# Cross-attention on one core: some scheduled steps moved to other tiles and engines, and the output projection of 14 batches done as three fp16 products

## The reference

```
q = (x @ Wq + bq).reshape(b, ql, H, D_Q)
k = (ctx @ Wk + bk).reshape(b, kl, H, D_Q)
v = (ctx @ Wv + bv).reshape(b, kl, H, D_Q)
scores = einsum('bqhd,bkhd->bhqk', q, k) / sqrt(D_Q)
attn = softmax(scores, axis=-1)
c = einsum('bhqk,bkhd->bqhd', attn, v).reshape(b, ql, H * D_Q)
z = x + (c @ Wo + bo)
out = (z - mean(z)) * rsqrt(var(z) + 1e-5) * gamma + beta
```

## Time and profile before

| | |
|---|---|
| three runs | 945.15 us median (942.49 to 946.78) |
| the profiled execution | 943.91 us, span of the trace 942.0 us |
| mean granted TensorE clock | 0.989 |
| PE busy | 892.3 us, 95% |
| DVE busy | 830.2 us, 88% |
| ACT busy | 754.6 us, 80% |
| POOL busy | 281.9 us, 30% |

### The profile page before, as it was taken

How to read it: one execution, slowest core, us unless ns; L and a number is a source line. 1 busy time by engine, 2 the same in 40 slices (tenths; PEclk the granted TensorE clock), 3 DMA queues, 4 the chain that set the end, 5 groups by cost and what they waited for, 6 DMA issues and landing times.

```text
span 942.0 us, 25453 instructions
## 1 busy us (share of the span) xinstructions
PE 892.3 (95%) x10366; PEld 673.4 (71%) x10366; DVE 830.2 (88%) x1072; ACT 754.6 (80%) x1082; POOL 281.9 (30%) x368
## 2 busy tenths in 40 slices
PE   7797998999999999999999999999999999999996
PEld 6475876777777776777777777777777676677775
DVE  4897889999898999989799998989999798998983
ACT  3675978888888888888888878888888888888983
POOL 3051394413214141232404223141412424042001
PEclk9998999999999999999999999999999999999999
DMA  8676999999999999999999999999999999999995
GB/s 224 133 159 143 186 175 163 204 203 187 220 181 205 201 214 205 201 213 183 208 198 206 211 178 211 193 215 201 197 212 192 198 196 196 198 183 203 204 178 112
DMA packets 683065, 181.17 MB, mean 192 GB/s; under 512 B 654596, under 2 KB 682052, under 8 KB 682948
## 3 DMA queue, kind: packets, MB, share of 16 engines
q1 hardware_dynamic: 681332, 178.48, 99.3%
q10 hardware_dynamic: 1344, 0.53, 0.2%
q0 software_dynamic: 272, 0.53, 0.2%
HBM read 15.35 MB, written 0.82 MB: 17 GB/s over the span
## 4 chain that ended last, share of the span: by engine, by line
PE 51%; DVE 22%; issue 8%; DMA 8%; POOL 5%; ACT 4%; SPq 1%; POOLq 0%; DVEq 0%; ACTq 0%
PE ps L530 21%; PE ps L544 15%; DVE p_lo L765 9%; PE ps L549 8%; DVE nmax L750 8%; DMA pt_lo<-p_lo 7%; PE ps L399 4%; PE ps L393 2%; DVE c_max L670 1%; ACT p L868 1%; POOL c_lo L975 1%; POOL early_sb L1003 1%; ACT c_hi L850 1%; POOL c_scaled L1001 1%; ACT o_t L891 1%
## 5 line engine op out<-in xcount | busy, mean ns | idle before, releaser
L765 DVE SCALAR_TENSOR_TENSOR p_lo<-p,rinv,p_hi 128x1444 f16<-128x1444 f32 x200 | 352.3, 1762 | 19.5 <-DMA pt_lo<-p_lo 17.2
L868 ACT ACTIVATE p<-ps,nmax 128x1446 f32<-128x1446 f32 x200 | 292.2, 1461 | 89.8 <-DVE nmax L750 89.1
L750 DVE TENSOR_REDUCE nmax<-ps 128x1 f32<-128x1446 f32 x200 | 331.5, 1658 | 36.3 <-PE ps L530 32.6
L876 ACT ACTIVATE p_hi<-p,rinv 128x1444 f16<-128x1444 f32 x200 | 299.8, 1499 | 39.0 <-DVE rinv L758 37.5
L544 PE MATMUL ps<-pt_hi,c_hi 128*128 128x128 f16 (+1 forms) x2288 | 270.0, 217 | 27.9 <-ACT o_t L891 25.2
L544 PEld LDWEIGHTS ps<-pt_hi,c_hi 128*128 128x128 f16 x2288 | 216.0, 98 | 76.2 <-ACT o_t L891 64.1
L544 PE MATMUL ps<-pt_hi,c_lo 128*128 128x128 f16 (+1 forms) x2288 | 269.3, 217 | 0.0
L544 PEld LDWEIGHTS ps<-pt_hi,c_lo 128*128 128x128 f16 x2288 | 217.5, 98 | 12.0 <-issue 0.2
L530 PE MATMUL ps<-ct_hi,g_hi 128*128 128x482 f16 (+3 forms) x624 | 157.2, 370 | 2.1 <-DMA ct_hi<-c_hi 2.1
L549 PE MATMUL ps<-pt_lo,c_hi 128*128 128x128 f16 (+1 forms) x2288 | 157.5, 217 | 0.0
L530 PE MATMUL ps<-ct_hi,g_lo 128*128 128x482 f16 (+3 forms) x624 | 157.1, 370 | 0.0
(11 more groups left out here) (108 smaller groups left out, 654.0 us busy)
## 6 DMA issues: line engine op xcount, KB each, us to landing
c_raw<-in_ctx_dram SPq DMA_DIRECT2D x32, 256.0 KB
pt_hi<-p_hi SPq DMA_TRANSPOSE x200, 3.5
pt_lo<-p_lo SPq DMA_TRANSPOSE x200, 3.7
c_raw<-in_ctx_dram SPq DMA_DIRECT2D x16, 192.0 KB
c_raw<-in_ctx_dram SPq DMA_DIRECT2D x48, 18.0 KB
out_dram<-y SPq DMA_DIRECT2D x16, 50.0 KB
x_sb<-in_x_dram SPq DMA_DIRECT2D x1, 600.0 KB
o_t<-in_L_xattn_Wq_dram SPq DMA_DIRECT2D x2, 256.0 KB, 4.4
```

What stands on the lines that cost most here:

```text
L750: dve.tensor_reduce(nmax[:, n % RING:n % RING + 1], ps[:, bank:bank + 3, 0:KEYW], AX.XY, ALU.max, negate=True).then_inc(s_nm, 1)
L765: dve.scalar_tensor_tensor(out=p_lo[:, par, 0:KL], in0=p32[:, n % P32S, 0:KL], scalar=rinv[:, i:i + 1], in1=p_hi[:, par, 0:KL], op0=ALU.mu ...
L868: act.activation(p32[:, n % P32S, :].rearrange("p (k w) -> p k w", w=KEYW), ps[:, bank:bank + 3, 0:KEYW], ACT.Exp, bias=nmax[:, i:i + 1], ...
L876: act.activation(p_hi[:, par, 0:KL], p32[:, n % P32S, 0:KL], ACT.Copy, scale=rinv[:, i:i + 1]).then_inc(s_hi, 1)
```

## The change

1. **Places.** CMAX_AT goes from 8 to 6. CHI_AT goes from 4, 5, 6 to 4, 6, 7. The context transposes go from r = 6 and 7 to 7 and 8, and the lo transpose to 9 in the first window only. TOP_AT goes from 11 to 10, except in the first window.
2. **Order on ACT.** `take_result(n-4)` is issued ahead of `exponentials(n)`.
3. **Engines.** The row norm (zn) goes from DVE to POOL. `context_scale` loses one small DVE instruction: the least maximum is a fourth column of `c_max`, and the range factor lies in a second identity, `ident_part`.
4. **Output projection.** For batches 1 to 14, `project_out_16` makes per head three fp16 products of a result (hi, lo) and `m_sb` (hi, lo) in place of one fp32 product. The result copy scales by a constant, and the scales are put back in `take_rows`. POOL splits each batch's result in four groups (`split_results`), between its splits of the queries. Once only, DVE takes the maxima of `m_sb` (n = 17 to 20, 22), ACT makes its high part (n = 23 to 26) and POOL its low part. `m16` and `o16` lie in the memory of `a_sb` and `xT`; the norm's tiles lie in that of `wo_sb`.

```
-    CHI_AT = 4
+    CHI_AT = (4, 6, 7)
-    CMAX_AT = 8
-    CT_HI_AT = 6
-    CT_LO_AT = 7
+    CMAX_AT = 6
+    CT_HI_AT = 7
+    CT_LO_AT = 8
+    CT_LO_AT_FIRST = 9
-    TOP_AT = 11
+    TOP_AT = 10
+    TOP_AT_FIRST = 11
...
+            def project_out_16(bank, heads):
+                for h in heads:
+                    rows = slice(QL * h, QL * (h + 1))
+                    for i, j in ((0, 0), (1, 0), (0, 1)):
+                        mm = pe.matmul(bank[0:QL, 0:D], o16[:, i, rows], m16[:, h, j, :], start=(h == 0 and i == j),
+                                       stop=(h == H - 1 and j == 1))
+                return mm
...
+                    if in_parts(w - 1):
+                        pe.wait_ge(s_os, NG * (w - 2) + g + 1)
+                        mm = project_out_16(bank, range(HG * g, HG * (g + 1)))
+                    else:
+                        mm = project_out(bank, (w - 1) % 2, range(HG * g, HG * (g + 1)))
...
-                dve.tensor_reduce(c_top[:, :], bank[:, 0:P], AX.X, ALU.max).then_inc(s_ctop, 1)
-                dve.wait_ge(s_ctop, b + 1)
...
-                dve.tensor_scalar(un, c_top[:, :], C_LEAST, 1.0 / C_RANGE, ALU.max, ALU.mult).then_inc(s_us, 1)
+                dve.tensor_reduce(un, bank[:, 0:P], AX.X, ALU.max).then_inc(s_us, 1)
...
+            def m_parts_max(g):
...
+                dve.tensor_reduce(m_parts[:, g:g + 1], m_sb[:, HG * g:HG * g + HG, :].rearrange("p h e -> p (h e)"), AX.X,
+                                  ALU.max, apply_absolute_value=True).then_inc(s_mp, 1)
...
+                if in_parts(b):
+                    dve.wait_ge(s_fu, b)
+                    dve.scalar_tensor_tensor(out=z[:, par, :], in0=ps[0:QL, JOB_BANK, 0:D], scalar=fin_un[0:QL, par:par + 1],
+                                             in1=x_sb[:, b, :], op0=ALU.mult, op1=ALU.add).then_inc(s_z, 1)
...
-                if r == TOP_AT and w > 0:
-                    norm_rows(w - 1)
...
             for n in range(N + LAG):
+                if n >= LAG:
+                    take_result(n - LAG)
                 if n < N:
                     exponentials(n)
-                if n >= LAG:
-                    take_result(n - LAG)
...
+                    act.activation(m16[:, HG * g:HG * g + HG, 0, :], m_sb[:, HG * g:HG * g + HG, :], ACT.Copy,
+                                   scale=m_scale[:, :]).then_inc(s_mh, 1)
...
+            def split_results(b, g):
+
+                pool.wait_ge(s_ot, results(b, HG * QL * (g + 1)))
+                if g == 0 and b > 1:
+                    pool.wait_ge(s_fin, b)
+                cols = query_columns(g)
+                pool.tensor_copy(o16[:, 0, cols], o_t[:, b % 2, cols]).then_inc(s_oh, 1)
+                pool.wait_ge(s_oh, NG * (b - 1) + g + 1)
+                pool.tensor_tensor(o16[:, 1, cols], o_t[:, b % 2, cols], o16[:, 0, cols], ALU.subtract).then_inc(s_os, 1)
...
+                        if w == 2:
+                            leave_m_lo(g)
+                        if g < NG - 1 and in_parts(w - 1):
+                            split_results(w - 1, g)
                         split_queries(b, g)
...
+                    split_results(w - 1, NG - 1)
+                    output_scale(w - 1)
```

More of the change, by code:

```diff
@@ L16 @@
 AX_RANGE = 2.0 ** 14
+O_PART = 2.0 ** -5
 P_RANGE = 2.0 ** 14
@@ L92, in halves, with results, in_parts @@
         return 16 * (n // 2 + 1)
+    def results(b, rows):
+        for n in range(first_tile(b), last_tile(b) + 1):
+            for i, (owner, row, count, at) in enumerate(segments(n)):
+                if owner == b and row + count >= rows:
+                    return segments_before(n) + i + 1
+    def in_parts(b):
+        return 0 < b < B - 1
     with ExitStack() as es:
@@ L118, in cross_attention_kernel @@
             "p (b i q) -> p b i q", i=2, q=QL)
-        wo_sb = sb("wo_sb", [P, PAIRS, P])
+        late_sb = sb("late_sb", [P, PAIRS, P])
+        wo_sb = late_sb
+        z, zn, zg, y = [late_sb[0:QL, 2 * i:2 * i + 2, :] for i in range(4)]
         bv_sb = sb("bv_sb", [P, PAIRS])
@@ L192, in cross_attention_kernel @@
         s_xres = sem("residual_ready")
+        s_mp = sem("m_group_max")
+        s_mc = sem("m_partition_max")
+        s_mt = sem("m_max_spread")
+        s_ma = sem("m_max")
+        s_mu = sem("m_unscale_ready")
+        s_ms = sem("m_scale_ready")
+        s_mh = sem("m_hi_ready")
+        s_mw = sem("m_scaled")
+        s_ml = sem("m_split")
+        s_oh = sem("result_hi_ready")
+        s_os = sem("result_split")
+        s_fu = sem("output_unscale_ready")
         s_axz = sem("ax_parts_zeroed")
+        s_cleast = sem("least_context_max_set")
         s_ax = sem("ax_group_max")
@@ L255, in cross_attention_kernel @@
         X16_AT = 18
+        MPARTS_AT = 17
+        MTOP_AT = IN_PAIR // 2 + TOP_AT
+        M16_AT = MTOP_AT + 1
         WARM_UP = 12
@@ L358, in _ @@
                     transpose_context_hi(w + 1)
-                if r == CT_LO_AT and w + 1 < B:
+                if r == (CT_LO_AT if w else CT_LO_AT_FIRST) and w + 1 < B:
                     transpose_context_lo(w + 1)
@@ L816, in _ @@
                     parts_max(n - PARTS_AT)
-                if r == TOP_AT and w > 0:
-                    norm_rows(w - 1)
-                if r == TOP_AT and w + 2 < B:
+                if r == (TOP_AT if w else TOP_AT_FIRST) and w + 2 < B:
                     context_scale(w + 2, ps[:, JOB_BANK, :])
@@ L903, in _ @@
                 w, r = window(n)
-                if CHI_AT <= r < CHI_AT + NT and w + 1 < B:
-                    context_hi(w + 1, r - CHI_AT)
+                if r in CHI_AT and w + 1 < B:
+                    context_hi(w + 1, CHI_AT.index(r))
                 for k in ONCE.get(n, ()):
@@ L1021, in _ @@
                     for g in range(NG):
+                        if w == 2:
+                            leave_m_lo(g)
+                        if g < NG - 1 and in_parts(w - 1):
+                            split_results(w - 1, g)
                         split_queries(b, g)
+                    if w == 2:
+                        pool.wait_ge(s_ml, NG)
+                if in_parts(w - 1):
+                    if b == B:
+                        for g in range(NG - 1):
+                            split_results(w - 1, g)
+                    split_results(w - 1, NG - 1)
+                    output_scale(w - 1)
+                if b < B:
                     if w == 1:
```

93 lines of the change are left out of this document (71 added, 22 removed).

## The result

The changed kernel takes **916.61 us** (median of 4 runs, 911.89 to 917.74), the kernel before 944.12 beside it (942.49 to 946.78). The ratio is 0.9696, with a 95% interval of 0.9655 to 0.9738: 27.5 us faster. The forecast was 927, in a range of 911 to 943. The profiled execution took 917.74 us, its span is 915.9, the mean granted clock 0.993.

What follows compares the result with a forecast made beforehand. PE was taken to bound the kernel, with 32 us lost to waits in the stretch. The terms -20 + 9 - 8 - 2 + 3 = -18 took 943.91 to 925.9, and 1.24 more for the median gave 927 us, range 911 to 943.

Steps and rivals of the forecast that it cites:

- Step 1: Result copy ahead of exponentials on ACT: DVE and ACT may lag about 2 us without stopping PE; -20 us (-32 to 0).
- what is late next: In the result copy's reordering: DMA lo transposes holding ACT's tail, 32.2 us in all, would be late next; lag absorbs part.
- Step 2: fp16 output projection on PE: twelve products with 100-column loads take 1.07 us against 0.91 for fp32 records; +9 us.
- 44 ns more makes at most 0.089: fp16 projection on PE: a 100-column load takes 44 ns more than a full one, so products follow at most 0.089 us apart.
- the end of -12: fp16 projection's fast end: products go by moving columns, 0.058 us each, the job takes 0.69 us, saving 12 us.
- Step 5: POOL's new result splits and norm: late query splits reach into p_lo on DVE, mostly covered by lag; +3 us (-1 to +18).
- Rival A: Narrow weight loads cost nothing, a projection product takes 0.058 us and ACT's chain leads: 918 us; chance 0.2.
- Step 3: First window: later lo transpose ends SP's 7.3 us stand for c_lo, which delays tiles 10 and 11; -8 us, or -4.
- Step 4: Second window: POOL's bias addition holds p_lo and PE stands 3.45 us; the lag absorbs about 2; -2 us (0 to -3.5).
- the uncovered end of 18: POOL's result splits delay query splits into p_lo at r = 2 and 3, 0.65 us each in 14 windows, uncovered: +18 us.
- Rival C: POOL takes the lead at r = 2 to 4: splits hold p_lo, DVE's tile there becomes 4.7 us; 955 us, chance 0.1.
- The moves: New places of maxima, scale and c_hi change when DVE and ACT are busy, not how much; counted at 0.

Runs made afterwards that it cites:

- fp32 out: The changed kernel with fp32 output projections for all batches and no result splits on POOL; the once-only fp16 weight preparation stays: 913.19 us, ratio 0.9697.
- Short splits: The changed kernel, but POOL splits 100 of each job's 400 result columns and all four heads' products read those: 904.77 us, ratio 0.9596.
- old places: The changed kernel with the places of windows 1 and later as before, the first window's new places kept: 923.47 us, ratio 0.9795.
- order back: The changed kernel with ACT's result copy issued behind the exponentials again, nothing else changed: 914.45 us, ratio 0.9708.
- order alone: The kernel before with only the result copy moved ahead of the exponentials on ACT: 929.12 us, ratio 0.9864.

## Why the prediction was right, and where its terms were not

The direction and the range were right, the forecast 10 us too high. That the total is so near is luck: its terms were off by 10 or 20 us, in both directions, and its largest gives nothing in the changed kernel.

**Step 1, -20.** DVE's lag (about 2 us) came as forecast. ACT's bare tile takes 3.77 instead of 3.89, and it is DVE that sets it. The mechanism exists: alone it gives 12 us, and 10 beside the new places with fp32 products. Beside the fp16 projection and the new places it gives nothing. The failed thought is in "what is late next": I named the DMA, which did not come (ACT's wait for it fell from 32.2 to 12.6 us), and not POOL's splits. PE still waits 42.5 us for the copy; with short result splits 23.7, with none and fp32 products 11.7. The copy also stands behind `hi_tail` and c_hi of the tile before now; what that costs was not tried apart.

**Step 2, +9.** As work of PE it is wrong in sign: "44 ns more makes at most 0.089". A longer record of a load was added to the pace of products, though the records overlap. The job takes 0.67 us, 56 x 0.24 = -13, just beyond the end of -12. As time it is worth nothing: steps 2 and 5 together stood at +12, and *fp32 out*, which takes both away, is between 0 and 3 us faster than the changed kernel. By the Trainium skill ("TensorE: Matmul & The Clock Gate", LDWEIGHTS) a plain load takes columns / 1.2 ns, which gives an estimate of 83 ns for 100 columns. That the products would follow at this pace is refuted by the same row, 56 ns. Whether the fast load is on with 100 columns no run shows; its record, 125 ns against 97, would say no, the pace says that it doesn't matter here. Rival A named this, and its 918 is near the result, but not by its sum, which has neither the places nor the splits' cost.

**Step 3, -8.** 67.3 us before, 60.9 after: -6.4. Tiles 10 and 11 take 11.3 us, not 10. Tile 10 still takes 6.69 us, 1.69 of them in wait for ACT's once-only copy to `m_sb`, for which it stood 4.98 before.

**Step 4, -2.** The second window took 65.7 and now 63.4 us, and PE's wait of 3.45 is gone. It is so in *fp32 out* too (64.2 us), where the addition holds p_lo for 5.15 us as before, which speaks for the lag. In the changed kernel the hold itself is shorter as well, 3.15 us.

**Step 5, +3.** Mis-sized. *Short splits* gives 9 to 12 us back, between the +3 and the uncovered end of 18. The place was right (query splits that reach into p_lo), but not the first half of the chain: that POOL's cast waits 1.5 us for a p_lo. And the cover by the lag of step 1 did not hold. By the Trainium skill ("GPSIMD Engine Reference", key points) GpSimd contends with VectorE instructions that have two SBUF inputs; the rows agree, 1.72 to 2.00 us. I used the rule in one direction only. Rival C had the mechanism, but not the place: tiles r = 2 to 4 take 4.28 to 4.36 us on average, not 4.7. The loss shows later: at r = 6 and r = 0, 4.95 and 4.29 us, against 4.55 and 4.02 in *short splits*. At r = 6 PE waits 0.72 us on average for the copy at its weight loads, in *short splits* 0.16; r = 0 lies beside the p_lo that the fourth result split holds.

**The moves, 0.** Wrong: 12 us alone, 7 beside the two others (*old places*). I asked what covers the maxima at their new place and not what their old place cost. That nmax was late at r = 10 to 0 stood in the trace of before.

**The sum.** By single parts, order -10, places -12, projection -8 and first window -6 make -36 before the second window is counted; -27.5 were measured. The eight stretches say which parts clash:

| projection, places | old order | new order | order gives |
|---|---|---|---|
| fp32, old | 716.1 | 705.9 | 10.2 |
| fp32, new | 703.6 | 691.9 | 11.7 |
| fp16, old | 708.0 | 704.7 | 3.3 |
| fp16, new | 695.5 | 697.5 | -2.0 |

With the old order, places (12.5) and projection (8.1) add up: 20.6 together. With fp32 products, order (10.2) and places (12.5) add up too: 24.2 together, although both take away PE's wait for the copy. Order and projection do not: 10.2 and 8.1 make 11.4 together, and beside the new order and new places the projection costs 5.6 (each stretch is that of one execution and can be off by 3; by the ratios of the whole times it costs nothing there). With short result splits it gives 5.9 there (686.0 against 691.9), so the full splits are what turns it. Why they hurt more in the new order stays open: the 200 p_lo take 367.4 us in *order back* as well. POOL's result cast starts inside a p_lo 39 times out of 56 in the new order and 13 times in the old one, but that this is the reason was not tried.

## What to carry to other kernels

Whether parts add up can't be read from which wait they remove: here two that cut the same wait added up, and one of them clashed with cheaper products on another engine. Test parts in pairs before their sum is believed. Before an operation is moved, look at how late its engine is at the old place, not only at the cover of the new one. Work given to an idle GpSimd isn't free if VectorE often reads two SBUF operands: either may stand for the other, and a copy of 0.5 us can take 2.

## What the runs showed of the hardware

- A weight load of 100 columns in fp16 has a record of 125 ns, one of 128 columns 97. Yet products follow each other every 45 ns with either: with the first if the moving side has 32 columns, with the second if it has 100. The record's length is not a pace.
- A POOL cast with one input, 128x400 from fp32 to fp16, takes 0.52 us alone and up to 2.03 when it starts beside p_lo; one of 128x100 takes 0.27 and up to 1.78. The stand, not the size, makes the time.
- A p_lo that starts while a two-input POOL instruction has time to go is not slowed but held: in the changed kernel it ends 1.51 to 1.53 us after that instruction, be it a subtraction of 128x400 (417.93 + 0.95, against 418.26 + 2.12) or the addition of 100x2048 (130.77 + 4.53, against 133.69 + 3.15); before too. Where a query split's subtraction had at most 0.13 us left, as in *order alone* and nearly always in *short splits*, p_lo kept its 1.71 us.
- An add of fp32 over 100x2048 on POOL that held a p_lo for 5.16 us before held one only until 3.15 us now, since it started 2.9 us ahead of it (130.77 against 133.69).
